# Moving VectorE's steps of a scan, one decay and one weight norm in a fused Macaron/Mamba kernel

## The reference

```python
x = x + 0.5 * ffn(layernorm(x))          # ffn: x @ W.T + lora/16 + bias, W from 4-bit groups
h = layernorm(x)                          # hidden of the block
h1 = rmsnorm(h, ln1_w)
z, xs, Bs, Cs, dt = split(h1 @ w_in.T)    # 512, 128, 128, 512, 4 columns
xs, Bs, Cs = silu(causal_conv4(xs, Bs, Cs) + conv_b)
dt = softplus(dt + dt_bias); a = -exp(A_log) * dt
# chunks of 128 tokens: cs = cumsum(a); Ldec = tril(exp(cs_q - cs_k))
Y = (C @ B.T * Ldec) @ (X * dt) + exp(cs) * (C @ state) + D * X
state = exp(cs_end) * state + (exp(cs_end - cs) * B).T @ (X * dt)
h = h + (Y * silu(z)) @ w_out.T
h2 = rmsnorm(h, ln2_w)
x = x + h + (silu(h2 @ gate.T) * (h2 @ up.T)) @ down.T   # inner width 1792
x = x + 0.5 * ffn(layernorm(x))
```

## Time and profile before

| | |
|---|---|
| median of 3 runs | 804.05 us (802.47 to 804.51) |
| profiled execution | 803.85 us, span 802.1 us |
| mean granted TensorE clock | 0.978 of full |
| busy in the span | PE 764.0 us (95%), DVE 636.7 (79%), ACT 444.2 (55%), POOL 336.1 (42%) |
| chain of work that ended last | PE 72%, DVE 14%, ACT 6%, issue 3%, DMA 3% |

### The profile page before, as it was taken

One profiled execution on the slowest core, in us unless ns is written; L12 is line 12 of the kernel. 1 busy time (PEld: TensorE's weight loads), 2 busy tenths in 40 slices (PEclk: granted clock), 3 DMA queues, 4 the chain that ended last, 5 costly groups with the idle time before them and its releaser, 6 DMA issues.

```text
span 802.1 us, 10670 instructions
## 1 busy us (share of the span) xinstructions
PE 764.0 (95%) x3480; PEld 354.5 (44%) x3480; DVE 636.7 (79%) x1246; ACT 444.2 (55%) x869; POOL 336.1 (42%) x392
## 2 busy tenths in 40 slices
PE   9978799899899989899999799999999999999998
PEld 4333355455445444344444344444444444444443
DVE  7789768777876886786889797787887888757994
ACT  3776567767666666454444545546545645534441
POOL 5513254454444348666523124325225224223674
PEclk9999899999999989899999999999999999999999
DMA  8923432542422111321060263554644644344564
GB/s 300 244 54 74 91 86 67 91 100 47 91 53 54 27 27 40 105 40 40 0 158 14 50 147 55 103 132 73 128 103 80 143 80 80 66 83 75 109 168 131
DMA packets 98166, 72.39 MB, mean 90 GB/s; under 512 B 67984, under 2 KB 75152, under 8 KB 98112
## 3 DMA queue, kind: packets, MB, share of 16 engines
q0 software_dynamic: 17280, 31.46, 22.0%
q1 hardware_dynamic: 80496, 40.20, 19.3%
q10 hardware_dynamic: 336, 0.05, 0.0%
HBM read 20.32 MB, written 4.19 MB: 31 GB/s over the span
## 4 chain that ended last, share of the span: by engine, by line
PE 72%; DVE 14%; ACT 6%; issue 3%; DMA 3%; POOL 1%; SPq 0%; ACTq 0%; DVEq 0%; POOLq 0%
PE PS L1898 61%; PE PS L2021 6%; DMA x_t<-hb 2%; DVE raw L1402 2%; DVE st L1234 1%; DVE stage L1402 1%; PE PS L2003 1%; DVE w_in L1311 1%; PE PS L2011 1%; PE PS L1994 1%; DVE xs L1334 1%; PE PS L1986 1%; ACT pre L846 1%; POOL r L512 1%; ACT th L856 1%
## 5 line engine op out<-in xcount | busy, mean ns | idle before, releaser
L703 POOL DMA_DIRECT2D xs<-x x59 | 51.0, 864 | 151.6 <-ACT x L1107 137.9
L1898 PE MATMUL PS<-h,w_in 128*128 128x512 f16 x480 | 109.0, 379 | 2.5 <-DMA h<-hn_p 2.1
L1898 PE MATMUL PS<-h,x_t 128*128 128x512 f16 x408 | 96.9, 388 | 3.2 <-DVE pre L1741 3.2
L1898 PEld LDWEIGHTS PS<-h,w_in 128*128 128x128 f16 x480 | 46.8, 98 | 68.2 <-issue 16.8
L1898 PE MATMUL PS<-n_T,stage 128*128 128x512 f16 x288 | 71.5, 379 | 0.0
L512 POOL TENSOR_TENSOR r<-mv,mhalf 128x1 f32<-128x1 f32 (+1 forms) x32 | 28.7, 897 | 91.6 <-DVE mv L1238 77.6
L1898 PEld LDWEIGHTS PS<-h,x_t 128*128 128x128 f16 x408 | 40.2, 100 | 54.1 <-issue 9.5
L1107 ACT ACTIVATE x<-PS,d_d 128x512 f32<-128x512 f32 x59 | 40.2, 681 | 38.6 <-PE PS L1898 38.6
L703 POOL DMA_DIRECT2D xs<-n x29 | 25.2, 869 | 72.9 <-ACT n L1107 62.6
L1898 PE MATMUL PS<-pre,stage 128*128 128x512 f16 x192 | 49.3, 379 | 0.0
L1077 ACT ACTIVATE xds<-tm,dgh 128x512 f32<-128x512 f32 x24 | 17.3, 722 | 55.1 <-DVE tm L1829 55.1
(11 more groups left out here) (306 smaller groups left out, 1795.4 us busy)
## 6 DMA issues: line engine op xcount, KB each, us to landing
xs<-x POOLq DMA_DIRECT2D x75, 256.0 KB, 3.3
xs<-n POOLq DMA_DIRECT2D x29, 256.0 KB, 3.2
x_t<-x_in SPq DMA_DIRECT2D x16, 256.0 KB, 3.6
x_t<-hb POOLq DMA_DIRECT2D x16, 256.0 KB, 3.8
out<-x_t SPq DMA_DIRECT2D x16, 256.0 KB, 2.3
raw_gu<-gate_t SPq DMA_DIRECT2D x7, 512.0 KB, 4.4
raw_gu<-up_t SPq DMA_DIRECT2D x7, 512.0 KB, 6.6
raw_d<-down_t SPq DMA_DIRECT2D x7, 512.0 KB, 7.4
```

The source lines that it names most:

```text
L703: po.dma_start(chunk_of(xs, c), d_tmps[d % 3], accum_op=ALU.add).then_inc(s_acc[d % 3], 16)
L1898: ins = pe.matmul(out_, lhs(a, b, k), rhs(a, b, k), start=first and n == 0, stop=last and n == len(todo) - 1)
```

## The change

Only the order of instructions moves; every operation stays. (1) In VectorE's prologue `x1_stats(4)` to `x1_stats(6)` stand earlier, `w_in_lo(2)` later, and `weights(0, 0)` and `scan1(0, 0)` ahead of the last `silu_z` and `lo1`. (2) In ScalarE's prologue `scan_decay(0, 0)` stands ahead of `hi1(7)` and `tanh_z(0, 3)`. (3) `gate_y(c)` gets its place step by step: earlier in steps 2, 6, 9, 10 and 11, later (behind `x1_stats`) in steps 3 and 7. `bound_row(0)` goes to the head of step 10. (4) In step 12 `cut_b` goes behind `gate_up(0, 0)` and `residual2(12)`. (5) `scales(2)` and `descale(2)` go from unit 2 into unit 1, and `norm(2)` from behind `tanh_s(2, 0)` to three places ahead of it.

```diff
@@ ScalarE, prologue
                 scan_ecs(0, 0)
                 scan1(0, 0)
+                scan_decay(0, 0)
                 hi1(7, 3)
                 tanh_z(0, 3)
-                scan_decay(0, 0)
                 scan2(0, 0)
@@ ScalarE, weight_work and unit
-                    if n == 2:
+                    if n == 2 and p > 1:
                         norm(p + 1, part)
...
                 if m > 0:
                     hi_s(m - 1, 0)
+                if m == 2:
+                    norm(2, 0)
                 copy_p1(m)
                 if m > 0:
                     hi_s(m - 1, 1)
+                if m == 2:
+                    norm(2, 1)
                 evict(ds[0])
+                if m == 2:
+                    norm(2, 2)
                 tanh_s(m, 0)
@@ VectorE, prologue
                 lo0(5, 1)
+                x1_stats(4, 0, PLAN["f", 4][0])
                 softplus(0, 0)
...
                 silu(0, 0)
-                w_in_lo(2)
-                x1_stats(4, 0, PLAN["f", 4][0])
                 prep0(6, 2)
+                x1_stats(5, 1, PLAN["f", 5][0])
                 taps(0, 2, 3)
                 silu(0, 1)
                 lo1(4, 0)
                 lo0(6, 2)
+                w_in_lo(2)
+                prep0(7, 3)
                 taps(0, 3, 6)
                 silu(0, 2)
-                x1_stats(5, 1, PLAN["f", 5][0])
-                prep0(7, 3)
                 taps(0, 4, 9)
                 silu(0, 3)
                 lo1(5, 1)
                 lo0(7, 3)
+                x1_stats(6, 2, PLAN["f", 6][0])
                 taps(0, 5, 12)
...
                 silu(0, 4)
-                x1_stats(6, 2, PLAN["f", 6][0])
                 prep0(8, 0)
...
                 prep0(9, 1)
+                weights(0, 0)
+                scan1(0, 0)
                 silu_z(0, 3)
                 lo1(7, 3)
-                weights(0, 0)
-                scan1(0, 0)
@@ VectorE, step
+                gate_mid = (j == 2 and a < NCH) or (a >= NCH and c <= 3 * CH and j != 2)
+                if c == 2 * CH + 2:
+                    bound_row(0)
+                if c == 2 * CH + 2 or c >= 3 * CH + 1:
+                    gate_y(c, j)
                 if late:
                     slot_a(i_late, late[0], {1: 3, 2: 12}.get(j))
...
+                    if gate_mid:
+                        gate_y(c, j)
                     for q in late[1:]:
                         slot_a(i_late, q, {1: 6}.get(j))
                     slot_b(i_late, late[0])
-                gate_first = a >= NCH or j == CH - 1
-                if gate_first:
-                    gate_y(c, j)
...
-                if c == 2 * CH + 2:
-                    bound_row(0)
-                if not gate_first:
+                if a < NCH and not gate_mid:
                     gate_y(c, j)
...
                 else:
-                    if j == 0:
-                        cut_b()
                     gate_up(0, j)
                 residual2(c, j)
+                if c == 3 * CH:
+                    cut_b()
@@ VectorE, unit
-                if m == 2:
-                    scales(2)
-                    descale(2)
...
                 if m == 1:
                     bound_row(2)
                     t_los(3, 0, 1, 2, 3)
+                    scales(2)
+                    descale(2)
```

## The result

| | before | changed |
|---|---|---|
| median (4 runs each) | 804.28 us (802.47 to 804.80) | 791.75 us (790.10 to 794.05) |
| ratio | | 0.985, 95% interval 0.9821 to 0.988 |
| profiled execution, its span | 803.85 us, 802.1 us | 794.05 us, 792.3 us |
| mean granted clock | 0.978 | 0.989 |

A forecast was written before the change was run, and what follows sets the result against it. TensorE was busy 95% of the span, so only its gaps and the low clock behind some could be won back. 6.0 + 2.1 + 1.2 + 3.2 + 0 = 12.5 us off 803.85 gave 791.4, range 787.9 to 794.8.

The forecast's parts named there:

- `f(7)` at full clock: Prologue: the low clock falls behind the gap at `f(6)`, leaving `f(7)` at full clock; 1.2 us counted of 1.6.
- the 0.8 us for `f(7)` starting sooner: Prologue: `hi0(7)` comes at 74.4, not 75.3, so `f(7)` starts near 82.8, not 83.5; 0.8 us.
- `scan_decay` and `scan1`, forecast at 4.0: Prologue: with the decay and first scan product moved ahead, `s2_diag(0)` starts 4.0 us earlier than 102.95.
- The prediction's own sign of being wrong: Prologue: the forecast would be wrong if `hi0(7)` isn't the last wait there; no size given.
- one of each: Steps 2 and 6: of the two new 1.95 us gaps, one draws a clock fall, one doesn't; 2.1 us gained.
- Rival (c): Whole kernel: VectorE doesn't hold TensorE back, so 20.3 us are gained, 783.6 us; chance 0.07.
- about 1 for the first product beside POOL: Unit 2: VectorE's first product beside POOL's additions costs about 1 us, set against 3.45 saved; pair 2 sums to 0.
- the rival (b): Units: pair 2's weights come sooner, unit 4 loses its gap and clock fall, 5.0 us, 786.4 whole; chance 0.14.
- (a): Whole kernel: the clock falls at each new gap, so only 8.1 us are gained, 795.8 us; chance 0.20.
- (d): Prologue: VectorE is late behind step 0, so the 6.0 us don't last; 6.5 gained, 797.4 us; chance 0.05.
- (e): Prologue: behind one 5 us gap the clock stays low for its rest, 15.5 us more, 806.9 us; chance 0.04.

The follow-up runs named there:

- lo7_early: The changed kernel with `lo1(5)` and `lo0(7)` ahead of `taps(0,4)` and `silu(0,3)`, `w_in_lo(2)` behind `silu(0,2)`; 791.44 us, ratio 0.9853 to before.
- no_pair2: The changed kernel with pair 2's scales, descale and norm put back where they were before; 790.85 us, ratio 0.9843 to before.
- adds_wait: The changed kernel with POOL's four additions of pair 2 waiting until VectorE's product behind `tanh_s(2, 0)` is done; 791.5 us, ratio 0.9856 to before.

## Why the prediction held, and where it did not

The time was right, 791.4 against 791.75, by parts that were not all of the right size. By stretches, for the two profiles first compared and for all of them (us gained):

| part | forecast | two profiles | all profiles |
|---|---|---|---|
| prologue | 6.0 | 1.6 (1.9 from the start) | 2.7 to 4.0 |
| steps 2 and 6 | 2.1 | 4.2 | 2.7 to 4.4 |
| steps 9 to 11 | 1.2 | 1.9 | 1.0 (means 50.5 and 49.6) |
| steps 12 to 15 | 3.2 | 3.0 | 3.0 |
| pair 2 and the units | 0 | -1.2 | -1.5 |

**Prologue: mis-sized.** Much came as described: `s2_diag(0)` at 96.9 to 99.8, one gap of 4.2 us ahead of `f(6)` in six of the seven profiles. Two terms failed. The 1.2 us for "`f(7)` at full clock": it took 4.45 us in three of the seven profiles of the changed prologue, and about 1.9 us of the way from `f(4)` to `s2_diag(0)` hang on that (51.5 to 52.0 us with it, 49.1 to 49.9 without). And the 0.8 us for `f(7)` starting sooner: it starts 34.5 to 35.7 us behind `f(4)` in the changed order and 34.7 to 36.3 in the old, so little of it is there beyond the profile of before, whose prologue was the slowest of its four, 1.8 us over their mean; the sum was made against that one. `scan_decay` and `scan1`, forecast at 4.0, measured 3 when alone (1.0 to 5.1 by the times, 3.2 by the stretch); the reordering of `x1_stats` and `w_in_lo(2)` brought nothing that times can show. The prediction's own sign of being wrong, that `hi0(7)` isn't the last wait of the prologue, came true in effect, as lo7_early tells: with `f(7)`'s wait gone, the sums that VectorE makes for `s1(0)` and POOL's mask were as late as before (`s1(0)` starts 41.5 us behind `f(4)`, in no_pair2 41.2), so a sooner `f(7)` is worth nothing.

**Steps 2 and 6: mechanism right, size off.** `w(2)` and `w(6)` lost their gaps and new ones came ahead of `proj(1,7)` and `proj(2,7)`, 1.4 us and not 1.95. The term mis-sized was "one of each" of falls: none of the 20 gaps of 1.4 us in ten profiles drew one. Against before's profile that is 4.2 us. Against the two profiles with old gates in which `w(2)` ran at full clock it is 2.7, of which 1.0 is gap (0.4 in step 2, where 0.17 us of wait came up behind the new gap, and 0.6 in step 6) and 1.7 the fall at `w(6)`. Four profiles with the old gates are too few to say what a typical run of before loses there.

**Steps 9 to 11.** The gap of step 10 became one of 2.56 us for `dA`, where before had 1.92 and 1.25 apart:

```profile
281.84 0.40 PE L1950 MATMUL PS<-dA,tri 128*128 128x16 f32 x2 [1.92 <-DVE dA L1553]
...
283.76 0.58 PE L2058 MATMUL PS<-mdg,ones 3*128 3x3 f32 x2 [1.25 <-DVE mdg L1442]
```

`w(10)` starts 1.1 us sooner against `w(8)`, forecast 1.2; the rest is the clock, which varies there by 1.6 us between profiles of one order.

**Steps 12 to 15: right.** 3.0 for 3.2, in every profile. TensorE first was 6.2 us ahead (`w(13)`), and 3.2 of it were gone by `w(15)`, by waits for POOL's mask and for `gate_y(15)`. Rival (c), VectorE doesn't hold TensorE back, falls here. `cut_b` itself took 2.8 us in its new place, forecast 3.4, and `scan1(14)` came 3.0 us sooner against `w(12)`, forecast 3.25.

**Pair 2: the term that was mis-sized is "about 1 for the first product beside POOL".** It was 3.55. Unit 4's gap and fall did go, as the rival (b) had it, and more than their price came back in unit 3 (1.2 us more in the two profiles, 1.5 in the mean of all, 0.7 where both orders had a fall). The size could have been read from the trace of before, one pair of MLP columns later, where TensorE has no gap for it. VectorE's product there starts 0.28 us behind POOL's second addition and is held for 3.06 us:

```profile
492.20 1.55 POOL L688 TENSOR_TENSOR stage<-raw_gu 128x512 f32<-128x512 f32 x1
492.48 3.06 DVE L1763 SCALAR_TENSOR_TENSOR S<-xds,S 128x512 f32<-128x512 f32 x1
493.42 1.55 POOL L690 TENSOR_TENSOR w_in<-w_in,raw_gu 128x512 f32<-128x512 f32 x1
```

It ends 0.57 us behind the third addition. So does every such product, and there are four in each of the fourteen profiles, besides the five of 4.24 us: 0.55 to 0.57 us behind the third. Held like these, a product that starts right behind the first addition costs about three of them, at 1.2 us from start to start, and not 1 us in all.

The Trainium skill (GPSIMD Engine Reference, section 8, Key points) says that GpSimd contends with VectorE instructions that have two SBUF inputs. adds_wait bears that out. By that rule alone unit 4 would have started 3.45 us sooner, as the prediction has it; what that leaves out is that the contention moved with POOL onto the two-input product that came next, and took 3.55 us there.

**Rivals.** (a) is wrong for the new gaps of 1.4 us, and right for that of 4.5 us in unit 3 (2.2 to 2.7 us for six matmuls, where 1.46 is full clock, in all five profiles that have it). (d): the prologue's gain did last, the stretch from `w(0)` to `w(8)` is the same to 0.04 us with either prologue. (e): the clock fell in the prologue up to three times and never stayed low for its rest.

One thing is open. The parts alone add up to 0.97% (0.04, 0.38, 0.40, 0.15), and the whole without pair 2 measured 1.57% less than before (1.2 to 1.94). The stretches show no stage in which the parts together do more than each alone, and four intervals of 0.2 to 0.26% each, taken together some 0.5%, could hide the difference; whether they do wasn't settled. By the stretches the change is worth 8 to 11 us (2.7 to 4.0, 2.7 to 4.4, 1.0, 3.0, less 1.5), by the two ratios 12.1 and 10.4. So the close agreement of 791.4 with 791.75 is luck: a prologue over-sized by 2 to 3 us and units over-sized by 1.5 stand against steps 2 and 6, under-sized by 0.6 to 2.3, and against a scatter of 1 to 2 us.

## What to carry to other kernels

Compare profiles by stretches between the same instructions of the pacing engine, over several executions and several variants: gaps then repeat to 0.1 us, and what is left is the clock and the start of the program, so that a part of 3 us in 800 can be told which whole times can't. A fall of the clock costs only where TensorE is the bound behind it (here 24 matmuls of 8.24 us or of 5.34 led to the same 57.6 us up to `w(15)`); price it from where the next wait ends, not from its own length. When work that contends with another engine is moved, look at which instruction stands beside it in its new place, and who waits for that one; then move what is late next in the same edit (here the weights' halves, 3.4 us, and 4.9 us together with `tanh_s(2, 0)`). Before taking a median's cause from a profile, look where that execution lies among the runs.
